# A three-layer decoder: twelve of sixteen mixture items computed by the chosen experts' rows alone, through indirect transfers, with a planned time row for every item

## What is computed

```python
x = _layernorm(x + attention(x))          # layer 0: causal self-attention, W_qkv, W_proj
x = _layernorm(x + cross_attention(x, ctx_1024, mask))   # layer 1: wq, wk, wv, wo
x = _layernorm(x + ffn(x))                # layer 2

def ffn(x):                               # TOP_K = 2, E = 8
    attn_out = unmasked self-attention of x (W_qkv, b_qkv)
    gate = jax.nn.softmax(x @ W_gate + b_gate, axis=-1)
    top_g, top_i = jax.lax.top_k(gate, TOP_K)
    combine = jnp.sum(jax.nn.one_hot(top_i, E) * top_g[..., None], axis=2)
    expert_out = jnp.einsum('bsd,edf->bsef', x, W_experts) + b_experts
    return attn_out + jnp.einsum('bsef,bse->bsf', expert_out, combine)
```

## Time and profile before

| | us |
|---|---|
| median of 3 runs | 900.43 |
| lowest and highest of them | 898.69, 901.26 |
| the profiled execution's own time | 899.34 |
| its span, first to last instruction | 897.5 |
| PE, DVE, ACT, POOL busy in the span | 868.2, 751.5, 587.0, 417.1 |
| mean granted share of TensorE's full clock | 0.993 |

### The profile page before, as it was taken

How to read it: one execution, slowest core, us unless ns; L and a number is a source line. 1 busy time by engine, 2 the same in 40 slices (tenths; PEclk the granted TensorE clock), 3 DMA queues, 4 the chain that set the end, 5 groups by cost and what they waited for, 6 DMA issues and landing times.

```text
span 897.5 us, 28533 instructions
## 1 busy us (share of the span) xinstructions
PE 868.2 (97%) x10018; PEld 747.9 (83%) x10018; DVE 751.5 (84%) x3509; ACT 587.0 (65%) x1211; POOL 417.1 (46%) x588
## 2 busy tenths in 40 slices
PE   7899999999999999999999999999999999999996
PEld 4688888888888898989888888888888888888874
DVE  3679887888888989888887888888888888888895
ACT  3678888788878878787878754454444444554533
POOL 7588888888874545454444321212222222222201
PEclk9899999999999999999999999999999999999998
DMA  5666566555544555444443221233333333333111
GB/s 176 166 178 174 147 175 167 151 164 153 146 121 126 138 129 138 115 131 121 125 115 102 68 75 54 65 84 84 84 84 84 84 85 84 84 84 83 47 51 37
DMA packets 98269, 100.58 MB, mean 112 GB/s; under 512 B 10705, under 2 KB 90705, under 8 KB 98129
## 3 DMA queue, kind: packets, MB, share of 16 engines
q1 hardware_dynamic: 98128, 98.77, 40.0%
HBM read 18.25 MB, written 4.19 MB: 25 GB/s over the span
## 4 chain that ended last, share of the span: by engine, by line
PE 86%; issue 7%; ACT 2%; POOL 2%; DVE 1%; DMA 1%; SPq 1%; ACTq 0%; POOLq 0%; DVEq 0%
PE work L512 45%; PE work L655 10%; PE max_scores L609 9%; PE scores L632 9%; PE work L664 4%; PE scores L635 3%; PE work L673 2%; PE work L537 2%; ACT attn L815 1%; PE work L518 1%; SPq L439 1%; PE work L620 1%; DMA q_stack<-neg_max_t 1%; PE max_scores L612 0%; DVE max_scores L982 0%
## 5 line engine op out<-in xcount | busy, mean ns | idle before, releaser
L815 ACT ACTIVATE attn<-scores 128x512 f32<-128x512 f32 x384 | 218.3, 597 | 112.2 <-PE scores L632 87.4
L982 DVE CUSTOM_DVE_ANT_0 max_scores<-max_scores,mask_qk 128x128 f32<-128x128 f32 x872 | 223.1, 324 | 28.8 <-PE max_scores L609 27.9
L1098 POOL TENSOR_TENSOR k_full<-k_full,k_parts 128x512 f32<-128x512 f32 x48 | 57.5, 1198 | 241.7 <-ACT k_parts L773 241.6
L609 PE MATMUL max_scores<-k_stack,q_stack 126*128 126x128 bf16 x1536 | 139.2, 221 | 10.7 <-DMA k_stack<-k_parts 5.7
L632 PE MATMUL scores<-q_stack,k_stack 128*128 128x128 bf16 x1536 | 138.7, 220 | 1.7 <-DMA q_stack<-neg_max_t 0.5
L1057 DVE SCALAR_TENSOR_TENSOR x_all<-work,combine,x_all 128x256 f32<-128x256 f32 x256 | 122.8, 481 | 10.2 <-PE work L512 5.3
L985 DVE TENSOR_REDUCE neg_max<-max_scores 128x4 f32<-128x512 f32 x166 | 110.5, 682 | 23.4 <-PE max_scores L609 20.1
L609 PEld LDWEIGHTS max_scores<-k_stack,q_stack 126*128 126x128 bf16 x1536 | 98.7, 98 | 36.9 <-issue 19.9
L982 DVE DVE_READ_ACCUMULATOR2_ANT neg_max<- 128x1 f32 x872 | 123.2, 141 | 0.0
L512 PE MATMUL work<-split_hi,w_hi 128*128 128x256 f32 x384 | 117.2, 305 | 0.9 <-DVE split_lo L884 0.8
L632 PEld LDWEIGHTS scores<-q_stack,k_stack 128*128 128x128 bf16 x1536 | 95.0, 98 | 25.8 <-issue 12.9
(11 more groups left out here) (126 smaller groups left out, 2030.1 us busy)
## 6 DMA issues: line engine op xcount, KB each, us to landing
k_stack<-k_parts SPq DMA_DIRECT2D x288, 128.0 KB, 2.5
q_stack<-q_parts SPq DMA_DIRECT2D x288, 128.0 KB, 2.5
in_t<-in_xt SPq DMA_DIRECT2D x16, 256.0 KB, 3.2
x_all<-in_x SPq DMA_DIRECT2D x16, 256.0 KB, 4.0
in_t<-in_ct SPq DMA_DIRECT2D x16, 256.0 KB, 3.4
out<-x_all SPq DMA_DIRECT2D x16, 256.0 KB, 2.4
stage<-in_e SPq DMA_DIRECT2D x4, 512.0 KB, 5.0
stage<-in_qk SPq DMA_DIRECT2D x2, 512.0 KB, 3.3
```

The lines of the kernel that those rows point to most:

```text
L609: mm = pe.matmul(dst[:, b, h2, :], head(QS, n, 2 * p + h2, b, ROWS), head(KS, n, 2 * p + h2, b, ROWS), start=(b + h2 == 0), stop=(b + h2 = ...
L815: act.activation(attn("exp", n, p)[:, :, :], SS[g % 2][:, :, :, :].rearrange("k b h q -> k (b h) q"), ACT.Exp).then_inc(probs_done, 1)
L982: ins = dve.tensor_tensor_reduce(scores, scores, MQ[l][:, :], -1.0, HUGE, ALU.add, ALU.min, NM[n % 2][:, b, h:h + 1])
L1098: pool.tensor_tensor(FULL[x][:, :, :], FULL[x][:, :, :], PART[x][:, 0, :, :], ALU.subtract).then_inc(rest_done[x], 1)
```

## The change

Items 32 to 43 become sparse; 44 to 47 stay dense. Three groups of four sparse items each do the following. DVE keeps a one-hot table of the two choices of every token (2048 rows a group). PE counts ranks in it (`rank`, 17 matmuls), and DVE turns them into a row number for each choice (`positions`), such that each expert's rows fill whole blocks of 128. POOL writes the token rows to these places in DRAM (16 indirect scatters of 128 rows). There are always 24 blocks, in 12 steps of two. SP loads a step's rows (256 KB). PE transposes them, ACT and DVE split them into high and low, PE multiplies with the weights of one expert a block, at an address out of a register, ACT copies the result, and SP stores it. POOL gathers the results back (16 indirect gathers), and DVE weighs and adds them (`weigh`). The DRAM rows are cleared once, early, by three DMAs on SP's queue (`clear_rows`, step `zfill`). Layer 2's end (bias, zadd, statistics, norm, store) of sparse items moves behind the group's gathers, and may be out of the items' order. `TIMES`, `PERIOD` and `SHIFTS` go; `ITEM_TIMES` has a planned time for each step of each item, in all three layers. The weights of all eight experts lie in one tensor, and some tensors share memory to make room. The diff, cut to its core:

```diff
+GROUP = 4
+GROUPS = 3
+DENSE = NITEM - NSTEP + GROUP * GROUPS
+CHOICES = 2
+COLUMNS = GROUP * PB * CHOICES
+PAIR_STEPS = (COLUMNS + E) // 2
+BLOCKS = 2 * PAIR_STEPS
...
-PERIOD = [16.58, 18.31, 28.89]
...
+ITEM_TIMES = {
...
+    9: {"in": [113.04], "xr": [144.07], "xh": [121.27], "xl": [120.36], "q": [126.28], "qe": [130.27], "qh":
+         [130.51], "qr": [133.24], "qm": [135.15], "ql": [139.74], "qs": [131.24, 138.64, 139.08], "k": [122.96],
+         "ke": [127.82], "kh": [128.01], "kr": [132.16], "km": [136.89], "kl": [140.98], "ks": [138.14, 143.14,
+         143.4], "v": [143.28], "va": [146.3], "s1": [142.31, 142.93, 146.29, 147.46, 148.08, 149.44, 150.61,
...
+    32: {
...
+         "mt": [508.44], "ml": [507.66], "s2": [510.3, 510.79, 511.41, 512.08, 517.11, 517.19, 517.82, 520.32],
...
+         [550.45], "cbt": [552.4], "bias": [557.04], "eb": [566.94], "zadd": [595.0, 583.42], "gat": [637.95, 639.08,
+         641.65, 642.26], "comb": [671.56, 674.53, 676.02, 677.0], "stat": [677.53], "rs": [654.24], "norm":
...
+    39: {
...
+         "rank": [614.91], "pos": [633.01], "scat": [630.32, 630.62, 630.95, 631.08, 631.41, 631.42, 632.32, 632.91,
+         633.18, 633.41, 633.64, 634.91, 636.08, 636.56, 636.73, 637.94], "gateT": [668.89], "cbt": [666.83], "bias":
...
+    42: {"xt": [646.13], "xh": [651.44], "xl": [650.58], "q": [653.91], "qe": [654.94], "qh": [656.09], "qr":
+         [644.07], "qm": [672.07], "ql": [644.57], "qs": [656.48, 675.08, 678.28], "k": [660.48], "ke": [663.73],
+         "kh": [665.4], "kr": [642.09], "km": [669.67], "kl": [644.18], "ks": [667.68, 672.59, 676.17], "v": [679.01,
+         684.12], "ve": [681.48, 684.7], "s1": [682.25, 687.08, 690.58, 690.63, 694.09, 695.67, 698.79, 701.32],
...
+ZFILL_TIME = 137.22
...
+            def clear_rows(n, part):
+                sp.wait_ge(setup_v, 1)
+                zeros = CBT[:, :].bitcast(F32).unsqueeze(1).to_broadcast([P, BLOCKS, D])
+                for j in range(REGIONS):
+                    sp.dma_start(XS[j].rearrange("(r p) d -> p r d", p=P), zeros).then_inc(rows_clear, 16)
+            def block_load(n, u):
+                j = step(n, u)
...
+                sp.wait_ge(scat_done, 16 * COLUMNS * (group(n) + 1))
+                if j >= 2:
+                    sp.wait_ge(btr_psum, j - 1)
+                sp.dma_start(BX[j % 2], XS[group(n)][2 * P * u:2 * P * (u + 1), :].rearrange("(h p) d -> p h d", p=P)).then_inc(bx_loaded[j % 2], 16)
+            def block_store(n, u):
+                j = step(n, u)
+                sp.wait_ge(bev_done, j + 1)
+                sp.dma_start(YS[group(n)][2 * P * u:2 * P * (u + 1), :].rearrange("(h p) d -> p h d", p=P), YB[:, :, :]).then_inc(y_stored, 16)
...
+            def rank(n, part):
+                chosen = MB[group(n) % 2]
+                pe.wait_ge(onehots, GROUP * (group(n) + 1))
...
+            def block_transpose(n, u):
...
+            def block_product(n, u):
...
+                if u % 4 == 0:
+                    _, regs = nc.values_load_multi_w_load_instructions(
+                        TAB[0:1, 2 * u:2 * u + 8], engines=[mybir.EngineType.PE], min_val=0, max_val=(E - 1) * EW,
...
+                pe.wait_ge(bl_done, j + 1)
+                dst, hi, lo = mine("bmm", n, u), BH[j % 2], BL[j % 2]
+                for h in range(2):
+                    r = chosen_expert[2 * (u % 4) + h]
+                    mm = three_pass(dst[:, h * D:(h + 1) * D],
+                                    lambda c: hi[:, c, h * P:(h + 1) * P], lambda c: lo[:, c, h * P:(h + 1) * P],
+                                    lambda c: WXH[:, bass.ds(r + c * D, D)], lambda c: WXL[:, bass.ds(r + c * D, D)])
...
+            def block_high(n, u):
...
+                act.activation(BH[j % 2], bank("btr", n, u)[:, :].rearrange("p (c n) -> p c n", c=C), ACT.Copy).then_inc(bh_done, 1)
+            def block_out(n, u):
+                j = step(n, u)
+                act.wait_ge(y_psum, j + 1)
+                if j:
+                    act.wait_ge(y_stored, 16 * j)
+                act.activation(YB[:, :, :].rearrange("p h d -> p (h d)"), bank("bmm", n, u)[:, :], ACT.Copy).then_inc(bev_done, 1)
...
+                if sparse(n):
...
+                    dve.tensor_copy(GTS[:, late(n), :, :], GT[:, :, 0:CHOICES])
+                    dve.tensor_tensor(MB[group(n) % 2][:, i:i + PB * CHOICES, :].rearrange("p (b k) e -> p b k e", k=CHOICES),
...
+            def positions(n, part):
...
+            def block_low(n, u):
...
+                dve.tensor_tensor(BL[j % 2], bank("btr", n, u)[:, :].rearrange("p (c n) -> p c n", c=C), BH[j % 2].bitcast(F32),
+                                  ALU.subtract).then_inc(bl_done, 1)
+            def weigh(n, part):
+                q, (b, k) = late(n), divmod(part, CHOICES)
+                x = pair(n)[:, b, :]
+                dve.wait_ge(gathered[q % 2], 16 * PB * CHOICES * (q // 2 + 1))
...
+                dve.scalar_tensor_tensor(out=x, in0=YG[q % 2][:, part, :], scalar=GTS[:, q, b, k:k + 1], in1=x,
+                                         op0=ALU.mult, op1=ALU.add).then_inc(comb_done, 1)
...
+            def scatter(n, part):
...
+                pool.indirect_dma_start(out=XS[j][:, :], out_offset=bass.IndirectOffsetOnAxis(ap=IDX[:, j, part:part + 1], axis=0),
+                                        in_=pair(n - GROUP + 1 + i)[:, b, :], in_offset=None).then_inc(scat_done, 16)
+            def gather(n, part):
+                q, j = late(n), group(n)
+                if part == 0:
+                    pool.wait_ge(y_stored, 16 * PAIR_STEPS * (j + 1))
...
+                pool.indirect_dma_start(out=YG[q % 2][:, part, :], out_offset=None, in_=YS[j][:, :],
...
```

507 lines of the change are left out of this document (423 added, 84 removed), and 319 rows, old and new, of tables (ITEM_TIMES, SHIFTS, TIMES).

## The result

The changed kernel took 1032.0 us (median of 4 runs, 1029.4 to 1039.0) where the kernel before took 900.6 in the same rounds (4 runs, 898.7 to 901.3): a ratio of 1.148, 95% interval 1.143 to 1.152. The prediction was 890 us, with a range of 850 to 926. Sign and range are both wrong. The profiled execution after took 1039.0 us, its span 1037.2.

The account below looks back on a forecast made before the run. PE, busy 97% of the span, was taken as the bound until DVE becomes the limit. From the 897.5 us span, -67 + 11 + 15 + 29 + 3 - 5 + 5 gave 888.5, with surroundings 890 us; range 850 to 926.

Parts of the forecast that it names:

- order, up to item 27: New planned order of all items: half of PE's 10.1 us idle between 40 and 300 us comes back, -5 us.
- clearing and the clock behind: Clearing DMAs on SP's queue delay the q and k copies behind them: +29 us PE idle, +3 for a slower clock.
- third layer up to PE's end: Third layer: PE matmul saving -67, register stops +11, DVE and PE queues waiting for each other +15 us.
- tail behind PE: End of the kernel: four sparse items wait for the last store, gathers and weighing, +5 us, between 0 and 15.
- Rival 1: The clearing is hidden by DMA sharing or SP's copies keeping their lead; 858 us, chance 0.20.
- PE's matmuls: Third layer: PE needs 24.1 us a group instead of 46.4, saving 67 us for three groups.
- Registers: Expert addresses from registers stop PE 0.25 us for each of 36 steps and 9 loads, +11 us.
- Rival 2: PE's sequencer becomes the bound because register work for each matmul isn't hidden; 933 us, chance 0.13.
- PE's other idle time: Third layer: the in-order queues of DVE and PE make each other wait, +15 us.
- rival 4: DVE is the limit, with its share no higher than 0.873 and more in the tail; 900 us, chance 0.10.
- POOL's transfers: 96 scatters and gathers at 1.2 us each, range 0.2 to 2.5, cost a mostly idle POOL 115 us, so nothing.
- rival 3: POOL's transfers hold up the next items, starting at 1.6 us each; 915 us at 2.2, chance 0.14.

Follow-up runs that it names:

- after_again: The changed kernel as it is, run again on another group's chip (chip 4): 962.5 us against 901.5 for the kernel before, ratio 1.069.
- order_only: The kernel before with the changed kernel's planned times for items 0 to 31, one run; `sum` of item 27 came at 469.9 us.
- static_expert: The changed kernel with each block's expert fixed at build time in place of registers PE reads from the table: 1033.1 us, ratio 1.151 to the kernel before.
- plain_pool: The changed kernel with its 96 indirect transfers replaced by plain POOL ones on fixed rows: 972.0 us against 901.5 for the kernel before, ratio 1.079.
- plain_padded: The changed kernel with plain fixed-row transfers, each followed by a POOL power and a wait for it: 969.8 us against 898.5 for the kernel before.
- clear_late: The changed kernel with the clearing cut into 36 transfers in the second layer, each group waiting for its own twelve: 939.4 us, ratio 1.046 to the kernel before.

## Why the prediction was wrong, point by point

The sum against the result's trace (+139.7 us of span) and against `after_again` (+61.3), both over the span before, 897.5:

```
term                           predicted   after   after_again
order, up to item 27                -5      +8.8      +8.8   (order_only)
clearing and the clock behind      +32     +29.3     +30.6   (item 6 to item 7, less order_only's 15.1)
rest of the first two layers         0      +4.3      +1.8
third layer up to PE's end         -41     +88.5     +10.4
tail behind PE                      +5      +8.8      +9.7
```

- **The clearing: right**, in mechanism and size, and in place to within 15 us. "+29 us of PE idle" was 27.4 us in one stretch, released by a copy into `k_stack`, and the granted clock of 140 to 200 us was 0.77 (0.64 from 182 to 188, as PE started again, and 1.00 from 188 to 200). The slow issues on SP were not in the working. Rival 1 fell. The remedy is shown as well: moving it into the second layer in 36 pieces gave back 20.6 us.
- **The order: wrong in sign**, +8.8 in one run (5 to 10 by the scatter of the old order) where -5 was taken. "An order can't give back more there, and could lose as much; I take half back" was a choice without a reason; the mean of its own bounds was nothing.
- **PE's matmuls: half of the saving came.** The added work was priced rightly: twelve block products took 1.42 us by the chain (1.48 predicted), four transposes 0.44. Yet from item 31's `sum` to its end PE was busy for 322.1 us in `after_again` and for 361.6 before: -39.5, not -67. An estimate of the rest: the granted clock over these 373.5 us was 0.96 (1.00 before), worth up to 15 us; and PE's work fell into 88 separate runs (3 before), each of which ends with a matmul of 0.28 us where the next start would have come after 0.12, some 14 us. Together they are of the size of the 27.5 us that are missing. Neither was tried by itself.
- **Registers: wrong in size**, +11 where `static_expert` shows nothing, to within some 8 us, and the gaps between the products differ by 1.2 us. Rival 2 fell with it. By the Trainium skill's floor for a tensor load (DMA: Bandwidth & Descriptors, Latency and other measured facts) 72 values unhidden were an estimated 43 us; the measurement decides against that use of it, since nine loads of eight cost less than some 8 us here.
- **PE's other idle time: the term that failed in every state.** "+15 us" for the two queues waiting for each other was 51.4 us of idle in the third layer of `after_again` (1.5 before), in short stops, 2.4 us the longest, for ACT's exponentials, DVE's subtractions, and transfers. DVE isn't the limit: it is busy for 300.6 of 391 us, 77%, so rival 4's mechanism fell too, and the stretch that by this term was to take 329 us at the dearest took 391. The step that failed is that work off PE counts "in full until DVE becomes the limit", with ACT's new work costed "at nothing" under the cover of its idle time. ACT's exponentials ended 9.3 us of PE's idle time there, and `block_out` 4.7. My reading, argued and not tried: a kernel in which a step goes out to DRAM and comes back (rows, blocks, block outputs, rows) has another limit, the length of its chain of waits in queues whose order is fixed, and I had costed those at nothing. A planned order that fits them badly would look the same. In `after_again`, `block_out` waited for the store before for 19.1 us, and the store's place in SP's queue for `block_out` for 82.2:

```profile
SPq L1029 <- ACT block_out L1451: 82.2, 25, 12.7
ACT block_out L1451 <- DMA expert_out<-block_out: 19.1, 8, 5.1
```

  Which of these waits is worth how much was not tried.
- **POOL's transfers: right in price, wrong in what they do.** 1.27 us each was near the 1.2 taken and under the 1.6 of rival 3. POOL's time costs nothing in this kernel (`plain_pool` against `plain_padded`), as the term said. Rival 3, which was to start at 1.6 us each, stayed away: `plain_padded` has 1.6 and is no slower than `plain_pool`. But held updates cost some 70 us, 1032.0 against 962.5 and 960.2. No row of before could show that, since there POOL issues no transfer; the range of 0.2 to 2.5 us covered the price of an instruction, not an effect on another engine's semaphores. This alone took the result from 7% slower to 15%.
- **The tail: +9 to +10** for +5, within its bounds of 0 to 15.

Without held updates the change would still have been 6.5 to 6.9% slower, outside the range and on the other side. The failure of the prediction doesn't hang on the held updates; its size does. The best variant, `clear_late`, is still 4.6% slower than before.

## What to carry to other kernels

Where one engine is busy for 97% of a span, don't count work taken off it in full if the work put in its place needs a new round trip: price the new chain (SBUF to DRAM, back, product, store, back) by its latencies beside the saved busy time. A small operation on a mostly idle engine can be what all else waits for: before an engine gets a burst of work, look at what stands behind it in its own queue, not at its share. Clear or preload large buffers in small pieces, and not ahead of copies that are read soon. And time a kernel with indirect transfers on more than one chip before judging it.

## What the runs showed of the hardware

- PE's semaphore updates can come up to 20.4 us late while POOL issues indirect transfers back to back (24.1 in `static_expert`), while of ACT's and DVE's that can be paired none is late. It is not always so: the same kernel took 1032.0 in the result's run, with late updates, and 962.5 and 960.2 on chip 4, without, while the kernel before took 898.4 to 901.5 everywhere.
- One indirect transfer of 128 rows of 1 KB keeps POOL for 0.96 us and 0.30 before the next; a plain one for 0.54 us with no gap. Sixteen in a row are 20.05 and 8.6 us.
- A matmul whose weight address is in a register costs no time that can be seen: starts are 0.118 us apart (median) with it and without.
- 9.44 MB in three transfers made PE wait 27 us for a copy behind them, and SP took 11.1 us to issue the next three copies instead of 1.83; the same bytes in 36 transfers in the second layer landed in 2.6 us each (median).
